# A gated graph network on one core: uneven legs, earlier messages, and a result finished by two engines

## The reference

```python
def step(h, _):
    messages = h[col] @ W_msg.T + b_msg
    agg = segment_sum(messages, row, num_segments=num_nodes)
    gi = agg @ W_ih.T + b_ih
    gh = h @ W_hh.T + b_hh
    r = sigmoid(i_r + h_r); z = sigmoid(i_z + h_z)
    n = tanh(i_n + r * h_n)
    return (1.0 - z) * n + z * h
out = layernorm(x + h_after_5_steps)     # over the 128 features, eps 1e-5
```

## Time and profile before

| | |
|---|---|
| median of three runs | 631.53 us |
| profiled execution, its own time | 631.4 us |
| its span | 629.6 us |
| TensorE busy | 576.4 us, 92% |
| VectorE, ScalarE, GpSimd busy | 54%, 51%, 45% |
| TensorE in the chain that ended last | 73% |
| granted TensorE clock, mean | 0.99 |

### The profile page before, as it was taken

How to read it: one execution, slowest core, us unless ns; L and a number is a source line. 1 busy time by engine, 2 the same in 40 slices (tenths; PEclk the granted TensorE clock), 3 DMA queues, 4 the chain that set the end, 5 groups by cost and what they waited for, 6 DMA issues and landing times.

```text
span 629.6 us, 8639 instructions
## 1 busy us (share of the span) xinstructions
PE 576.4 (92%) x3077; PEld 328.1 (52%) x3077; DVE 342.7 (54%) x735; ACT 321.6 (51%) x571; POOL 285.0 (45%) x397
## 2 busy tenths in 40 slices
PE   4568888887999999999999999999999999999991
PEld 3455555554455555556545555655555655555550
DVE  2679999996577523236623433742323571354556
ACT  3558888887444533445444444543334553443442
POOL 5012222221300575665557776466665555666600
PEclk9998999999999999999999999999999999999997
DMA  6023657666000000000000000000000000000012
GB/s 172 8 54 96 127 117 124 119 124 110 1 0 1 1 1 0 1 1 0 1 2 1 1 0 1 0 1 1 0 2 0 1 1 1 1 0 1 1 33 73
DMA packets 32222, 18.56 MB, mean 29 GB/s; under 512 B 4658, under 2 KB 31257, under 8 KB 32177
## 3 DMA queue, kind: packets, MB, share of 16 engines
q1 hardware_dynamic: 29050, 13.91, 10.8%
q0 software_dynamic: 1856, 3.90, 2.5%
q10 hardware_dynamic: 1270, 0.16, 0.3%
HBM read 2.84 MB, written 1.60 MB: 7 GB/s over the span
## 4 chain that ended last, share of the span: by engine, by line
PE 73%; DMA 9%; DVE 6%; ACT 5%; issue 3%; SPq 2%; DVEq 0%; ACTq 0%
PE PS L753 39%; PE PS L730 8%; PE PS L734 8%; DMA A<-stage 8%; PE PS L573 4%; PE PS L741 4%; PE PS L740 4%; PE PS L671 3%; SPq L471 2%; ACT spread L956 2%; ACT stage L944 1%; DVE y L1154 1%; PE PS L662 1%; DMA bmsg<-in_L_gnn_b_msg 1%; DVE parts L1113 1%
## 5 line engine op out<-in xcount | busy, mean ns | idle before, releaser
L537 POOL CAST ring<-A 128x896 f16<-128x896 uint8 (+4 forms) x324 | 249.1, 808 | 196.0 <-PE PS L753 182.9
L753 PE MATMUL PS<-ring,parts 128*128 128x448 f16 x1372 | 270.8, 352 | 2.0 <-DVE parts L1113 2.0
L753 PEld LDWEIGHTS PS<-ring,parts 128*128 128x128 f16 x1372 | 133.6, 98 | 128.2 <-issue 10.7
L1306 DVE SCALAR_TENSOR_TENSOR pre_n<-PS,small,gate_r 128x448 f32<-128x448 f32 x35 | 23.9, 683 | 207.3 <-PE PS L741 207.2
L1007 ACT ACTIVATE ring<-A 128x896 f16<-128x896 uint8 (+4 forms) x144 | 105.8, 773 | 0.1
L990 ACT ACTIVATE gate_r<-PS,small 128x448 f32<-128x448 f32 x35 | 22.2, 633 | 145.2 <-PE PS L734 145.2
L671 PE MATMUL PS<-spread,parts 128*128 128x448 f16 x294 | 73.3, 357 | 12.1 <-ACT spread L956 12.0
L956 ACT ACTIVATE spread<-A 128x1056 f16<-128x1056 uint8 (+1 forms) x75 | 70.8, 949 | 18.4 <-DMA A<-stage 18.3
L528 POOL DMA_DIRECT2D A<-stage x50 | 26.6, 531 | 112.6 <-ACT stage L944 112.6
L662 PE MATMUL PS<-hot_row,hot_key 128*128 128x132 bf16 x588 | 52.5, 225 | 9.6 <-DVE hot_row L1269 8.9
L662 PEld LDWEIGHTS PS<-hot_row,hot_key 128*128 128x128 bf16 x588 | 45.6, 127 | 29.7 <-ACT stage L944 15.3
(11 more groups left out here) (142 smaller groups left out, 500.6 us busy)
## 6 DMA issues: line engine op xcount, KB each, us to landing
A<-stage SPq DMA_DIRECT2D x150, 66.0 KB, 3.3
A<-stage POOLq DMA_DIRECT2D x50, 66.0 KB, 3.1
y<-in_x SPq DMA_DIRECT2D x3, 256.0 KB, 6.6
y<-in_x SPq DMA_DIRECT2D x2, 384.0 KB
out<-y SPq DMA_DIRECT2D x4, 192.0 KB, 2.4
out<-y SPq DMA_DIRECT2D x3, 256.0 KB, 2.2
edges_dst<-in_dst SPq DMA_DIRECT2D x1, 195.3 KB
w_raw<-in_L_gnn_W_ih SPq DMA_DIRECT2D x1, 192.0 KB
```

Source lines behind the costliest of these rows:

```text
L537: last = nc.gpsimd.tensor_copy(to, data)
L753: mm = pe.matmul(PS[:, AGG_BANKS[(t * LEGS + b) % 2], 0:LW], parts[:, k, part, :], ring[:, SLOT_OF[at_piece] % SLOTS, k % 2, :], start=(k ...
```

## The change

Steps 1 to 4 use legs of 480 columns, six of them, and a last one of 256; step 0's product keeps its seven banks of 448, but its gates follow the new legs. The number of matmuls, casts and pieces stays as it was. Message positions move, the gates in the last leg stand ahead of piece 3, nine units are made between the gates of step 0. In step 4, groups 0 to 3 are deviated at the end of ScalarE's leg 5 and normalised ahead of the chain of leg 5; groups 4 and 5 (tiles 15 to 21) are normalised by ScalarE (`norm_too`) with a scale and a bias that VectorE makes (`scales`), and group 6 has three tiles instead of four.

```diff
-GATES_AT_END = 4
+GATES_AT_END = 3
+    LONG = 480
-        ring = later.next("ring", [P, SLOTS, 2, LW], F16)
+        ring = later.next("ring", [P, SLOTS, 2, LONG], F16)
+        def cols(b):
+            return min(LONG, NP - b * LONG)
         def span(flat, b):
-            return flat[:, b * LW:(b + 1) * LW]
+            return flat[:, b * LONG:b * LONG + cols(b)]
-        IN_FIRST = {2: (0,), 4: (1, 2), 6: (3, 4)}
+        IN_FIRST = {2: (0,), 3: (1, 2), 4: (3, 4), 5: (5, 6), 6: (7, 8)}
+        IN_FIRST_ALL = 9
         AT_PIECE = {7: (10,), 8: (11,), 9: (12,)}
-        AT_PIECE_FIRST = {1: (5,), 2: (6,), 3: (7,), 6: (8, 9), 7: (10,), 8: (11,), 9: (12,)}
+        AT_PIECE_FIRST = {1: (9,), 2: (10,), 7: (11,), 8: (12,)}
         def leg_of(p):
-            return min(p, NP - 1) // LW
+            return min(p, NP - 1) // LONG
         def late_units(t):
-            return range(5 if t == 1 else EARLY + 2, UNITS)
+            return range(IN_FIRST_ALL if t == 1 else EARLY + 2, UNITS)
-        ENDS = [0] + [min((b + 1) * LW // P, KT) for b in range(LEGS - 1)] + [KT]
+        ENDS = [0] + [min((b + 1) * LONG // P, KT) for b in range(LEGS - 1)] + [KT]
+        DONE_SOONER = range(LEGS - 3)
+        BY_SCALAR = range(LEGS - 3, LEGS - 1)
+        TILES_BY_SCALAR = range(QUADS[BY_SCALAR[0]][0], QUADS[BY_SCALAR[-1]][-1] + 1)
...
@@ SyncE, the stores of the result
-                sp.wait_ge(res_made, RES_DONE[b])
+                if b in BY_SCALAR:
+                    sp.wait_ge(res_by_act, RES_DONE[b] - RES_DONE[BY_SCALAR[0] - 1])
+                else:
+                    sp.wait_ge(res_made, RES_DONE[b] - (len(TILES_BY_SCALAR) if b > BY_SCALAR[-1] else 0))
...
@@ TensorE, step(t)
-                            if b == LEGS - 1 and not last and 1 <= e <= EARLY:
-                                message(t + 1, e - 1)
+                            if b == LEGS - 1 and not last and e < EARLY:
+                                message(t + 1, e)
...
@@ ScalarE
+            def norm_too():
+                act.wait_ge(scales_made, 1)
+                for k in TILES_BY_SCALAR:
+                    nc.scalar.activation(y[:, k, :], y[:, k, :], ACT.Identity, bias=less_mean[:, k, :],
+                                         scale=rstd[:, k, :]).then_inc(res_by_act, 1)
...
-                    if t == 1 and b == 0:
-                        for u in range(5, EARLY):
-                            high_part(t, u)
...
                     if b == 0:
-                        for u in range(EARLY if t == 1 else EARLY + 2, UNITS):
+                        for u in late_units(t):
                             high_part(t, u)
                     expand(t, b, BY_ACT[3])
-                    if b == LEGS - 1 and last:
-                        deviation(range(LEGS - 3))
+                    if b == LEGS - 2 and last:
+                        deviation(DONE_SOONER)
...
                 candidate(t, b)
-                deviation(range(LEGS - 3, LEGS))
+                deviation(BY_SCALAR)
+                norm_too()
+                deviation((LEGS - 1,))
...
@@ VectorE
+            def scales():
+                a, z = TILES_BY_SCALAR[0], TILES_BY_SCALAR[-1] + 1
+                dve.wait_ge(std_made, BY_SCALAR[-1] + 1)
+                nc.vector.reciprocal(rstd[:, a:z, 0], std[:, a:z, 0]).then_inc(rstd_made, 1)
+                dve.wait_ge(rstd_made, len(DONE_SOONER) + 1)
+                nc.vector.scalar_tensor_tensor(out=less_mean[:, a:z, 0], in0=mv[:, a:z, 0], scalar=-1.0, in1=rstd[:, a:z, 0],
+                                               op0=ALU.mult, op1=ALU.mult).then_inc(scales_made, 1)
...
                     if last:
+                        norm(DONE_SOONER)
                         before_tanh(t, b - 1)
                         after_tanh(t, b - 1)
                         statistics(b - 2)
-                        norm(range(LEGS - 3))
                         statistics(b - 1)
...
                 for t in range(1, STEPS):
                     step(t)
+                scales()
                 statistics(LEGS - 1)
-                norm(range(LEGS - 3, LEGS))
+                norm((LEGS - 1,))
```

More of the change, by code:

```diff
@@ L102, in gnn_kernel @@
     assert (KT - 1) % 2 == 0 and LW * LEGS == NP <= PLANES * WORDS and LW <= BANK and LW % 2 == 0
+    assert LONG <= BANK and 0 < NP - (LEGS - 1) * LONG <= LONG
     assert CW == HIGH * LOW and LOW % DUP == 0
@@ L176, in gnn_kernel @@
         later = Row(AT_WORK)
[L177 removed]
+        ring = later.next("ring", [P, SLOTS, 2, LONG], F16)
         def work(name):
[L180 removed]
+            return later.next(name, [P, LONG], F32)[:, :]
         gate_r, pre_n, cand = work("gate_r"), work("pre_n"), work("cand")
@@ L718, in gates @@
                     hb = span(hT[:, :], b)
-                    gb = agg[b % 2] if t else span(first[:, :], b)
+                    w = cols(b)
+                    gb = agg[b % 2][:, 0:w] if t else span(first[:, :], b)
                     if done == 0:
@@ L729, in gates @@
                     for g, bank in enumerate((R_BANK, Z_BANK)):
-                        pe.matmul(PS[:, bank, 0:LW], wT[:, 3 + g, :], hb, start=True, stop=False)
+                        pe.matmul(PS[:, bank, 0:w], wT[:, 3 + g, :], hb, start=True, stop=False)
                     if t:
@@ L733, in gates @@
                     for g, bank in enumerate((R_BANK, Z_BANK)):
-                        mm = pe.matmul(PS[:, bank, 0:LW], wT[:, g, :], gb, start=False, stop=True)
+                        mm = pe.matmul(PS[:, bank, 0:w], wT[:, g, :], gb, start=False, stop=True)
                     mm.then_inc(rz_made, 1)
@@ L739, in gates @@
                         pe.wait_ge(pre_ready, done)
-                    pe.matmul(PS[:, HN_BANK, 0:LW], wT[:, 5, :], hb, start=True, stop=True)
-                    pe.matmul(PS[:, IN_BANK, 0:LW], wT[:, 2, :], gb, start=True, stop=True).then_inc(n_made, 1)
+                    pe.matmul(PS[:, HN_BANK, 0:w], wT[:, 5, :], hb, start=True, stop=True)
+                    pe.matmul(PS[:, IN_BANK, 0:w], wT[:, 2, :], gb, start=True, stop=True).then_inc(n_made, 1)
                 for b in range(LEGS):
@@ L752, in product @@
                         for part in range(last):
-                            mm = pe.matmul(PS[:, AGG_BANKS[(t * LEGS + b) % 2], 0:LW], parts[:, k, part, :],
-                                           ring[:, SLOT_OF[at_piece] % SLOTS, k % 2, :],
+                            mm = pe.matmul(PS[:, AGG_BANKS[(t * LEGS + b) % 2], 0:cols(b)], parts[:, k, part, :],
+                                           ring[:, SLOT_OF[at_piece] % SLOTS, k % 2, 0:cols(b)],
                                            start=(k == 0 and part == 0), stop=(k == KT - 1))
@@ L1079, in _ @@
                         nc.scalar.activation(cand[:, 0:FB], pre_n[:, 0:FB], ACT.Tanh, bias=bih[:, 2:3]).then_inc(gs_cand_ready, 1)
-                deviation(range(LEGS))
-            act.wait_ge(res_made, KT)
+                deviation(range(LEGS - 1))
+                norm_too()
+                deviation((LEGS - 1,))
+            act.wait_ge(res_made, KT - len(TILES_BY_SCALAR))
             nodes, tile = last_tile(out, y)
@@ L1317, in times_z @@
                     dve.wait_ge(d_made, done + 1)
-                    nc.vector.tensor_tensor(diff, gate_z[done % 2], diff, ALU.mult).then_inc(zd_made, 1)
+                    nc.vector.tensor_tensor(diff[:, 0:cols(b)], gate_z[done % 2][:, 0:cols(b)], diff[:, 0:cols(b)], ALU.mult).then_inc(zd_made, 1)
                 def new_h(t, b):
                     dve.wait_ge(zd_made, t * LEGS + b + 1)
-                    nc.vector.tensor_tensor(span(hT[:, :], b), cand, diff, ALU.add).then_inc(h_ready, 1)
+                    nc.vector.tensor_tensor(span(hT[:, :], b), cand[:, 0:cols(b)], diff[:, 0:cols(b)], ALU.add).then_inc(h_ready, 1)
                 def after_tanh(t, b):
@@ L1415, in _ @@
                     statistics(g)
-                norm(range(LEGS))
+                norm(DONE_SOONER)
+                scales()
+                norm((LEGS - 1,))
 _INS = ['x', 'src', 'dst', 'L0_gnn_W_msg', 'L0_gnn_b_msg', 'L0_gnn_W_ih', 'L0_gnn_W_hh', 'L0_gnn_b_ih', 'L0_gnn_b_hh']
```

25 lines of the change are left out of this document (13 added, 12 removed).

## The result

Over 16 runs of each kernel on the same chips the changed kernel took 635.08 us (632.73 to 637.08) where the kernel before took 632.42 (630.26 to 634.66): a ratio of 1.0044, interval 1.0032 to 1.0056, or 2.8 us slower. Forecast were 634.4 us and 2.9 us slower. The profiled execution took 636.11 us, with a span of 634.3.

The account below looks back on a forecast made before the run. The prediction took TensorE's work, busy 92% of the span, to bound the kernel. From 631.4 us, -0.9 + 3.9 - 0.1 = +2.9 gave 634.3, and 634.4 for the median of runs, range 629.8 to 637.2.

Parts of the forecast that it names:

- TensorE's work does not change: All products and gates: 480-wide and 256-wide legs total 64.9 us of products and 31.6 of gates a step, as before.
- Step 0 into step 1: Where step 1's product begins: holes of 2.1 us against 3.0 before, so -0.9 us (bounds -2.5 and +0.5).
- The three later boundaries: Last legs of later steps: TensorE's messages 6 and 7 wait for VectorE; three times 1.3, +3.9 us (+1.8 to +5.6).
- G: Time mark in a step's last leg: the end of the gates there, from which message times are counted.
- my lower bound: At a later boundary: a loss of 0.6 us if the multiplication by z took 0.63 us instead of 1.35.
- The hole at piece 11 stays: Later boundaries: same chain through ScalarE, +0.05 us, against two pieces 0.1 longer, so the hole remains.
- The last step: Step 4's end: a new stall against a shorter finish, summing to -0.1 us (bounds -1.5 and +1.2).
- X: Time mark in the last step: the end of leg 4's gates in leg 5, 38.3 us before the end.
- the stall: Ahead of piece 2 of leg 6 in step 4: TensorE waits 1.7 us for ScalarE's cast behind group 3's root.
- VectorE is not in TensorE's way: Faster rival: multiplication by z under 0.75 us at the boundaries, total 631.5 us; chance 0.25.
- Contention spreads: Slower rival: casts hit three operations instead of one, 1.9 us a boundary, 2.2 at leg 6, total 636.9; chance 0.13.
- The table load: Rival at the end: Identity not in the root's table, two loads of 1.28 us, total 637.0; chance 0.03.

Follow-up runs that it names:

- Experiment 5: Changed kernel with GpSimd's casts for the first ten pieces of leg 0 in steps 2 to 4 cut to 64 columns: steps of 103.84, 103.83 and 103.85 us.
- experiment 10: Kernel with uneven legs only in steps 0 and 4, later roots and join messages; ScalarE's cast for piece 11 ahead of its high parts: 627.47 us, ratio 0.9928.
- Experiment 3: Changed kernel with ScalarE's roots of groups 0 to 3 put behind its first cast of leg 6: 634.35 us against 631.79, ratio 1.0031.
- experiment 1: Changed kernel with VectorE's message 5 ahead of the multiplication by z and message 6 ahead of the new state: 642.61 us against 631.79, ratio 1.0165.
- experiment 2: Changed kernel with TensorE's messages 5, 6 and 7 later, behind pieces 6, 8 and 10 of the last leg: 643.27 us against 631.79, ratio 1.0168.
- experiment 4: The whole change except the legs, which stay seven equal ones of 448: 633.4 us against 631.79, ratio 1.001.
- experiment 9: Changed kernel with experiment 1's VectorE order and the narrow casts of experiment 5 together: 103.81 us for each step, one run of 636.13.

## Why the prediction came out right

**TensorE's work does not change: right.** Products follow each other at 0.11 us for 256 columns (four in 0.44), gates of the short leg take 2.64 (308.23 to 310.87) where 2.60 was put. All 1372 products are busy for 270.4 us where they were for 270.8.

**Step 0 into step 1: right.** Forecast -0.9, measured -0.8. Message 9 waited as foreseen, for VectorE in the short leg's chain: TensorE's timeline of the changed kernel.

```profile
202.76 1.13 PE L588 MATMUL PS<-wT,hT 128*128 128x128 f32 x8 [0.20 <-DVE msg_later L1124]
...
207.09 0.68 PE L588 MATMUL PS<-wT,hT 128*128 128x128 f32 x4 [1.52 <-DVE msg_later L1124]
```

The hole is 1.5 where 2.0 was put, with 0.2 ahead of message 7 that was not foreseen; the hole at piece 11 is gone from this leg.

**The three later boundaries: right in place and mechanism, too small in size.** Forecast 1.3 each, measured 1.74, so 1.3 of the total is missing here. Read from start to start, with G = 299.51: TensorE would have been ready for message 7 at G+3.8 (put at 3.96); VectorE's message 5 ended at G+5.3 (put at 5.2) and TensorE started 0.14 after that (put at 0.1). The 3.96 was too late by a reading: the prediction has message 7 of the kernel before at 300.60, a sum counted from the modelled end of the gates, where its row starts at 300.44, so the slack was 0.4 and not 0.55. And every wait costs more than its idle time says. Message 6 started 0.48 after its turn (302.91 instead of 302.43) and message 7 1.09, where the idle column has 0.33 and 0.93, and each then held the next instruction 0.08 longer (0.52 against 0.44 from start to start). The operation that met the cast was not the one that I named. I kept 1.35 for the multiplication by z because it had that value before, "since the casts of 480-wide pieces still start as slots come free in that stretch"; they do, but the low part of 3 was hit and the multiplication was free. The sum came as near as it did by luck: either waits for the rest of one cast. Experiment 5 prices this: the loss without casts in the way is about 0.91, not the 0.6 of my lower bound.

**The hole at piece 11 stays: right** (0.45 against 0.50). The prediction put it down to a chain through ScalarE without naming the cast; it was the cast, and not the low part that the page names (experiment 10).

**The last step: right in mechanism, 0.8 too dear.** Forecast -0.1, measured -0.9. With X = 602.16, the stall ended at X+7.75 (put at 8.1) and was 1.37, not 1.7, since VectorE's statistics of group 3 ended at X+6.8 instead of 7.2; 0.4 of the 0.8 was already gained when the two roots ended, at X+24.1 instead of 24.5. The seven activations took 0.39 each from start to start (629.47 - 626.76 over seven; put at 0.39) and the rest of the end ran at the spacing foreseen; the store took 3.2 after its issue where 3.5 was put. Experiment 3 shows the stall to be worth 1.4 us at the end. VectorE's norms of groups 0 to 3 ended at X+11.6 (put at 12). The prediction's sentence on norms at twice their time ("about 1 us late") does not follow from its own figures, by which they would end at X+16.7 against 13.4; it did not come to that, since one cast of 0.40 was all that ran beside them (four tiles 1.24 there, 1.12 elsewhere). The Trainium skill, "ScalarE: Activation LUTs" (Table sets: the hidden batching unit), on cheap functions in every set, agrees: Identity came without a load between the root and it.

**The rivals.** *VectorE is not in TensorE's way* fell: the condition that it set, the multiplication under 0.75 us, did hold (0.65), and still VectorE was late, so the condition named a single operation where it should have named the chain. *Contention spreads* put 1.9 on a boundary, and the measured 1.74 is nearer to that than to the forecast's 1.3; but its condition, three operations hit, did not hold ahead of message 7, where only the low part of 3 was. Experiments 1 and 2 went beyond it, to 3.7 to 5.3 us a boundary (106.65 to 108.23 against 102.93), the clock's share included. The table load did not come.

The two errors, 1.3 us too little at the boundaries and 0.8 too much at the end, partly cancel. The forecast of the total was better than that of its terms, and part of that is luck.

## What to carry to other kernels

An operation that shares a port with another engine does not cost a factor more but the rest of what runs there, so its price hangs on the moment at which it starts, and a change of order that looks free on its own engine must be laid over the other engine's starts first. A change that lets the busiest engine run ahead also frees its helpers sooner; in experiment 2 they then ran together in another engine's way, and holes grew until the clock fell, which cost more than the hole that was to be closed. Uneven legs paid here where a chain was exposed, at the start and the end of the loop, and cost where the chain was just covered; they need not be the same in every step. And a releaser named in a profile is a guess where two events end together: move one of them and look.

## What the runs showed of the hardware that was not expected

The clock. In the changed kernel, holes of 1.5 us and less left the granted clock at 1.00. In experiment 1 the last leg of each step had TensorE busy for only about 60% of six microseconds. Its windows (bounds: length, busy us and instructions by engine, granted clock, DMA):

```profile
305.00:311.00 6.00, 3.65 (x30) 3.32 (x31) 5.79 (x9) 1.61 (x4) 4.38 (x4) 1.00 0.00 0
411.50:417.50 6.00, 3.51 (x30) 3.17 (x30) 5.78 (x9) 1.45 (x4) 4.45 (x4) 1.00 0.00 0
417.50:422.00 4.50, 4.50 (x15) 3.33 (x14) 1.70 (x5) 3.84 (x8) 0.00 (x0) 0.62 0.00 0
```

The first stretch was followed by full clock. The second, nearly the same, was followed by 0.62 over the short leg's gates: mostly the lower level, 1.2 GHz, and four gate matmuls took 2.08 us instead of 1.03. It cost that step 1.6 us (108.23 against 106.65). In experiment 2 a fall came at each of the three boundaries, to 0.57 in 309 to 311 at the first. In experiment 4, 4.24 busy us of six at the join, with holes of 0.67, 1.10 and 0.82, were followed by 0.50 over 2.5 us, although none of these holes is as long as the 1.5 that left the changed kernel's clock alone. In experiment 9, which has the order of experiment 1 without the holes, the clock over 417 to 422 was 1.00. Why the first and the third of experiment 1's boundaries kept the clock and the second lost it stays open. The clock's share was 1.6 us of one step in experiment 1, some 1.3 at a boundary in experiment 2, 1.4 at the join in experiment 4.
